# Fetching six tiles of expert outputs and one matrix a stage earlier in a two-layer recurrent and expert kernel

## The chip, the cores and the metric

The kernel runs on one core of one Trainium2 chip. The metric is the device time of one execution in microseconds (us). Engines are named as in the profile: PE (TensorE), PEld (its weight loads), DVE (VectorE), ACT (ScalarE), POOL (GpSimd), SP (SyncE, here a queue for DMAs). Engines tell each other of finished work by semaphores: an instruction or a DMA adds to one, and a queue waits until it has reached a number.

## The reference

Input x has 8 sequences of 512 tokens with 128 features. There are two layers of the form x = x + s * silu(f), both branches from the normalized x.

```python
xn = _layernorm(x)
s = _L0_attn_ref(xn, ...)      # Mamba block: scan, projection, RMS norm, MLP with GELU, RMS norm
g = _silu(_L0_ffn_ref(xn, ...))  # 24 experts, top 2, two expert layers, then layer_norm(out + xn)
x = x + s * g
xn = _layernorm(x)
s = _L1_attn_ref(xn, ...)      # causal attention, 8 heads
g = _silu(_L1_ffn_ref(xn, ...))  # 128 experts, top 2
x = x + s * g
```

The parts at hand are, in layer 0, the end of the Mamba block and the combination of the second expert layer's outputs:

```python
return jnp.einsum('bld,ed->ble', y, out_proj_w)      # end of _mamba
Z_mam = _rmsnorm(y + Z, norm1_w)
h = jax.nn.gelu(jnp.einsum('bld,fd->blf', Z_mam, mlp_w1) + mlp_b1, approximate=False)
return _rmsnorm(jnp.einsum('blf,df->bld', h, mlp_w2) + mlp_b2 + Z_mam, norm1_w)
...
return jnp.einsum('sec,ecf->sf', combine, h)         # end of moe_apply: two rows of two experts per token
...
return layer_norm(out + x, ln_out_w, ln_out_b)
```

## The kernel before

Tokens lie in NT = 32 tiles of P = 128; a batch b (one sequence) has TB = 4 tiles. The program is a row of stages (blocks). In a block each engine has a queue of its own, written as a generator; a block ends when all its engines are through, and only then does the next begin. `side_by_side(main, beside)` weaves two generators on one queue: at each `yield` of the main one it runs the second to its next `yield`, and what is left of the second comes at the end. So the number of `yield`s sets the order of instructions on a queue.

The stages that matter here:

- The scan stage (`scan_stage` with `Moe0Experts` beside it, about 100 to 842 us). DVE scans; PE, ACT, POOL and SP also run both expert layers. SP's queue ends with the stores of expert outputs to `y2_dram` (L1177) and a wait for them (L1180). POOL's queue ends with the gathers of the second layer's inputs (L1222).
- The output stage (`mamba_output_stage` with `Moe0Output` beside it, 842.6 to 1014.6 us). SP loads nine weights (L1512), the normalized rows `xn` in eight parts (L1515) and x (L1516). First phase, b = 0 to 7: PE projects batch b into the one bank `p_o` (L723), DVE adds the rows (L826), which frees the bank, ACT takes squares and roots, DVE scales batch b-1 (L811, L813). After each b DVE combines one pair of tiles: weighted sum of the two gathered rows and the bias product (L1612, L1615), plus `xn`, statistics (L1619 to L1626). PE makes the bias product of four tiles (L1560) after every second projection. Second phase, b = 0 to 7: turn, MLP with GELU, second product, again with one pair of tiles beside each. The end: DVE scales the four quarters of `s_rows` (L811, L813), computes the scale of the second half of the expert branch (`scales(1)`, L1603, L1604), ACT centres it (L1575) and takes SiLU (L1594), DVE weighs (L1639, L1641) and makes the products with s and x (L1648, L1649).
- POOL gathers in that stage, two indirect DMAs for each tile (L1527), into a ring of four tiles `yk`; tile t waits until tile t-4 is combined. PE, ACT and DVE wait for all weights before anything else, POOL before its second tile pair.
- The attention stage (`attention_stage` with `Moe1` beside it, 1057 to 1624 us). 64 heads, two steps each. Beside them run the 128 experts of layer 1; POOL then gathers their outputs (L2220, ring of eight tiles), DVE combines pairs at the steps that begin with `COMBINE_STEP`, ACT takes SiLU at `SILU_STEP`, and from `FINAL_STEP` on DVE makes the final products.

The memory of the rows (`state`) is shared: words 0 to 10752 are the experts' arena during the scan stage, and words 8192 to 12288 are `s_rows`, written in the second phase.

## Time and profile before

| | us |
|---|---|
| median of 3 runs (1626.17 to 1627.29) | 1626.33 |
| the profiled execution: its own time | 1628.29 |
| its span | 1626.5 |
| PE busy | 1348.3 (83%) |
| DVE busy | 1243.7 (76%) |
| ACT busy | 851.8 (52%) |
| POOL busy | 644.9 (40%) |

The span runs from the first instruction to the last. A profile is one execution, and its own time is some microseconds off the median. Busy shares are means over all stages. In a timeline a bracket gives the idle time of the engine before the instruction and what ended it; "issue" is nothing that the profile shows, "remote" an unknown releaser. Ends of matmuls are modelled. PEclk 1.00 is TensorE's granted clock of 2.4 GHz, 0.50 is 1.2 GHz.

### The profile page before, as it was taken

The page shows a single profiled execution, that of the slowest core. Times are in us where ns is not written, and L with a number is a line of the kernel's source. Part 1 is how long each engine was busy: PE and PEld are TensorE (multiplying, and loading weights), DVE is VectorE, ACT ScalarE, POOL GpSimd, SP SyncE. Part 2 cuts the span into 40 slices and gives each one's busy share as a digit, 9 for nine tenths or more (in the row PEclk, how much of TensorE's full clock was granted, in tenths as well). Part 3 has the DMA queues.
Part 4 walks back from the last instruction along what each step waited for, and adds up shares of the span by engine and source line. Part 5 has one row for each costly group of instructions (what it writes and reads, how often), then busy time and mean ns, then how long its engine had stood idle before and what let it go on. Part 6 is the DMA issues. An engine that isn't in the chain of part 4 may idle for free. (4 is left out here: it accounts for less than half of the span.)

```text
span 1626.5 us, 21868 instructions
## 1 busy us (share of the span) xinstructions
PE 1348.3 (83%) x7560; PEld 918.1 (56%) x7560; DVE 1243.7 (76%) x2259; ACT 851.8 (52%) x2096; POOL 644.9 (40%) x592
## 2 busy tenths in 40 slices
PE   7968787879878569898955791589999999798998
PEld 5524444434434348787845561556677677565676
DVE  6669999988898999999956447558887555466667
ACT  5366565656968736565512464743553444333353
POOL 0035655226988664546315440049300221355000
PEclk9978999979898679999977896899999999899999
DMA  6013544443444124545423010300010322112001
GB/s 207 0 30 108 140 137 128 131 135 105 130 129 125 58 80 133 143 126 142 115 77 113 26 27 0 107 1 1 1 53 7 85 82 82 33 36 38 6 14 39
DMA packets 75891, 127.31 MB, mean 78 GB/s; under 512 B 11758, under 2 KB 38606, under 8 KB 75174
## 3 DMA queue, kind: packets, MB, share of 16 engines
q1 hardware_dynamic: 56326, 75.04, 15.3%
q0 software_dynamic: 19456, 50.88, 11.8%
q8 instruction: 61, 1.00, 0.2%
q14 instruction: 48, 0.39, 0.1%
HBM read 85.51 MB, written 40.37 MB: 77 GB/s over the span
## 5 line engine op out<-in xcount | busy, mean ns | idle before, releaser
L643 DVE TENSOR_TENSOR_SCAN sc_st<-sc_dA,sc_st 128x1024 f32<-128x1024 f32 x128 | 293.1, 2330 | 0.0
L2042 DVE COPY at_pT<-at_p_t 128x512 f32<-128x512 f32 (+1 forms) x192 | 109.5, 599 | 147.9 <-PE at_p_t L1935 126.8
L1993 ACT ACTIVATE at_pr<-at_p_s,at_nmx 128x512 f32<-128x512 f32 (+3 forms) x256 | 131.4, 526 | 145.6 <-DVE at_nmx L2019 142.7
L1191 POOL DMA_INDIRECT g_state<-xn_scratch,moe_tab x96 | 116.4, 1212 | 183.0 <-POOLq L99 102.2
L613 DVE TENSOR_TENSOR sc_st<-sc_u,sc_p_b 128x1024 f32<-128x1024 f32 x128 | 154.8, 1210 | 43.2 <-PE sc_p_b L483 20.2
L422 ACT ACTIVATE sc_dA<-sc_dt,g_state 128x511 f32<-128x511 f32 x256 | 169.1, 710 | 16.2 <-DVE sc_st L643 12.7
L1914 PE MATMUL at_p_s<-att_xaT,at_qT 128*128 128x512 f32 (+3 forms) x512 | 175.1, 464 | 0.0
L1948 PEld LDWEIGHTS at_p_o<-at_V,at_pT 128*128 128x128 f32 x1280 | 152.3, 192 | 31.3 <-issue 30.4
L1222 POOL DMA_INDIRECT g_state<-r_scratch,moe_tab x96 | 119.8, 1248 | 108.2 <-PE e_bank L1321 74.1
L1948 PE MATMUL at_p_o<-at_V,at_pT 128*128 128x128 f32 x1280 | 153.8, 275 | 3.1 <-DVE g_state L2032 3.1
L621 DVE TENSOR_TENSOR sc_st<-sc_st,sc_p_c 128x1024 f32<-128x1024 f32 x128 | 155.0, 1211 | 0.0
L513 PEld LDWEIGHTS sc_p_y<-g_ident,sc_st 128*128 128x128 f32 x1024 | 133.9, 154 | 32.6 <-issue 22.1
L513 PE MATMUL sc_p_y<-g_ident,sc_st 128*128 128x128 f32 x1024 | 148.8, 294 | 3.3 <-DVE sc_st L621 3.3
L2019 DVE TENSOR_REDUCE at_nmx<-at_p_s 128x1 f32<-128x512 f32 (+3 forms) x256 | 109.5, 481 | 38.2 <-PE at_p_s L1917 28.1
L483 PE MATMUL sc_p_b<-sc_bc,mamba_sel 96*128 96x512 bf16 x128 | 55.7, 435 | 94.1 <-DVE sc_st L613 86.8
L1201 POOL DMA_INDIRECT g_state<-y_scratch,moe_back x64 | 87.3, 1364 | 84.0 <-DMA y_scratch<-g_state 51.6
L1935 PE MATMUL at_p_t<-g_ident,at_pr 128*128 128x128 f32 x640 | 94.2, 279 | 25.4 <-ACT at_pr L1993 13.1
L1935 PEld LDWEIGHTS at_p_t<-g_ident,at_pr 128*128 128x128 f32 x640 | 75.2, 143 | 65.5 <-DVE at_pT L2042 29.5
L1273 PE MATMUL e_bank<-g_state 128*96 128x512 f32 x192 | 101.6, 631 | 8.0 <-ACT g_state L1335 6.1
L1308 PE MATMUL e_bank<-g_state 128*96 128x128 f32 x768 | 102.2, 277 | 4.4 <-ACT g_state L1442 4.0
L2210 POOL DMA_INDIRECT f_xg<-xn_scratch,l_tab x32 | 30.3, 946 | 184.6 <-DVE l_tab L2418 92.3
L1914 PEld LDWEIGHTS at_p_s<-att_xaT,at_qT 128*128 128x128 f32 x512 | 79.1, 193 | 42.3 <-issue 40.4
(299 smaller groups left out, 2697.6 us busy)
## 6 DMA issues: line engine op xcount, KB each, us to landing
y_scratch<-g_state SPq DMA_DIRECT2D x24, 768.0 KB
g_state<-W SPq DMA_DIRECT2D x48, 256.0 KB
r_scratch<-g_state SPq DMA_DIRECT2D x16, 512.0 KB, 2.6
y_scratch<-g_state SPq DMA_DIRECT2D x24, 192.0 KB
xn_scratch<-g_state SPq DMA_DIRECT2D x16, 256.0 KB, 4.5
g_state<-x SPq DMA_DIRECT2D x4, 512.0 KB, 6.8
g_state<-xn_scratch SPq DMA_DIRECT2D x8, 256.0 KB, 4.6
g_state<-x SPq DMA_DIRECT2D x1, 2048.0 KB, 12.8
```

What stands on the lines that cost most here:

```text
L422: ins = nc.scalar.activation(dA[:, m % 4, j, 1:L], dt[:, b % 2, h, 1:L], ACT.Exp, scale=negA[:, h, 2 * q + j:2 * q + j + 1])
L513: ins = nc.tensor.matmul(p_y[:, t, h * P:(h + 1) * P], st[:, (2 * i + h) % RS, j, t * P:(t + 1) * P], w["ident"], is_transpose=True, start ...
L613: nc.vector.tensor_tensor(st[:, m % RS:m % RS + 2, j, :], u[:, b % 2, :, :], p_b[:, :].unsqueeze(1).broadcast_to([P, HALF, L]), ALU.mult). ...
L621: nc.vector.tensor_tensor(st[:, m % RS, :, :], st[:, m % RS, :, :], p_c[:, :, :], ALU.mult).then_inc(hc_ready, 1)
L643: nc.vector.tensor_tensor_scan(st[:, m % RS, :, :].rearrange("p a b -> p (a b)"), dA[:, m % 4, :, :].rearrange("p a b -> p (a b)"), st[:, ...
L1191: nc.gpsimd.indirect_dma_start(out=self.xg[:, e % 4, h, :], out_offset=None, in_=self.xn_rows, in_offset=bass.IndirectOffsetOnAxis(ap=r.ta ...
L1222: nc.gpsimd.indirect_dma_start(out=self.rg[:, e % 3, h, :], out_offset=None, in_=self.r_rows, in_offset=bass.IndirectOffsetOnAxis(ap=r.tab ...
L1914: nc.tensor.matmul(p_s[:, bank, c:c + K], qT[:, n % 3, i * P:(i + 1) * P], xaT[:, b, 0:K], start=True, stop=False)
L1935: ins = nc.tensor.transpose(p_t[:, bank, c + (i - j) * P:c + (i - j + 1) * P], pr[:, n % 2, sbank, sc + j * P:sc + (j + 1) * P], w["ident"])
L1948: ins = nc.tensor.matmul(p_o[:, i, :], pT[:, n % 2, bank, c + (i - j) * P:c + (i - j + 1) * P], V[:, b % 2, j, h * D:(h + 1) * D], start=( ...
L1993: ins = nc.scalar.activation(pr[:, n % 2, bank, c:c + K], p_s[:, bank, c:c + K], ACT.Exp, bias=nmx[:, n % 2, i:i + 1], accum_out=sums[:, n ...
L2019: ins = v.tensor_reduce(nmx[:, n % 2, i:i + 1], p_s[:, bank, c:c + (i + 1) * P], AX_X, ALU.max, negate=True)
```

## The change

- The memory: a new class `Ahead` takes words 8192 to 10752 of `state`, in which the experts' arena is free once the last outputs are stored: the projection's matrix `out_T` (two tiles) and six tiles of pairs of expert output rows.
- The scan stage: behind the wait for the last stores SP loads `out_T`, and POOL, behind the same waits, issues 12 gathers (tiles 0 to 5).
- The output stage: PE's first wait is for `out_T` alone. The wait for the other eight weights stands before PE's first bias product, before ACT's first GELU work, and on DVE behind the first L826. SP loads two parts of `xn` first, then the weights, then the other six parts. POOL gathers tiles 6 to 27 into a ring of eight without a wait for weights, weighs its first quarter, gathers tiles 28 to 31, and weighs the other three. DVE yields once behind the first quarter of `s_rows`, so that `scales(1)` comes there and no longer behind all four.
- The attention stage: combination begins at step 84, not 80; SiLU at 110, not 108.

```diff
@@ -714,7 +714,7 @@
         block = ctx.enter_context(nc.Block())
 
         def tensor_steps(pe):
-            pe.wait_ge(beside.weights_in, 16 * len(beside.weights))
+            pe.wait_ge(beside.ahead.out_in, 16)
             for b in range(B):
                 if b:
                     pe.wait_ge(o_used, b)
@@ -756,7 +756,6 @@
                 yield
...
         def scalar_steps(act):
-            act.wait_ge(beside.weights_in, 16 * len(beside.weights))
             link = Chain(act, a_chain)
...
@@ -776,6 +775,7 @@
                 roots(slice(b * TB, (b + 1) * TB))
                 yield
             yield
+            act.wait_ge(beside.weights_in, 16 * len(beside.weights))
             for b in range(B):
                 act.wait_ge(z_turned, b + 1)
...
@@ -800,8 +800,6 @@
         def vector_steps(dve):
             link = Chain(dve, chain)
             nc.vector.memset(eps[:, :], 1e-6).then_inc(eps_set, 1)
-            dve.wait_ge(beside.weights_in, 16 * len(beside.weights))
-
...
@@ -824,6 +822,8 @@
                     dve.wait_ge(beside.xn_in[b], 16)
                     dve.wait_ge(projected, b + 1)
                     nc.vector.tensor_tensor(z[:, t, :], rows(p_o), xn_rows[:, t, :], ALU.add).then_inc(o_used, 1)
+                if b == 0:
+                    dve.wait_ge(beside.weights_in, 16 * len(beside.weights))
                 if b:
                     dve.wait_ge(root_ready, b)
...
@@ -841,6 +841,8 @@
             for c in range(4):
                 t = slice(c * 8, (c + 1) * 8)
                 scale(s_rows[:, t, :], t, s_ready)
+                if c == 0:
+                    yield
...
@@ -856,7 +858,7 @@
 
         @block.gpsimd
         def _(pool):
-            side_by_side((None for _ in range(2 * B + 1)), beside.pool(pool))
+            beside.pool(pool)
...
 
+class Ahead:
+
+
+    TILES = 6
+
+    def __init__(self, scope, w, rows, out_T):
+        out_rows = rows[:, 0:HALF * D].rearrange("p (a b) -> p a b", b=D)
+        w["out_T"], self.out_T = out_rows, (out_rows, out_T)
+        self.yk = rows[:, 8 * D:(8 + 2 * self.TILES) * D].rearrange("p (t k d) -> p t k d", k=2, d=D)
+        self.gathered, self.out_in = scope.sem("ahead"), scope.sem("out_in")
+
+
...
     def sync(self, sp):
@@ -1178,6 +1193,7 @@
                          self.out2[:, e % 2, :, :]).then_inc(self.stored2[e % 2], 16)
         for i in range(2):
             sp.wait_ge(self.stored2[i], 16 * (E0 // 2))
+        sp.dma_start(*self.ahead.out_T).then_inc(self.ahead.out_in, 16)
 
     def pool(self, pool):
         nc, r = self.nc, self.r
@@ -1246,6 +1262,14 @@
         for e in range(E0):
             gather_r(e + self.AHEAD)
             yield
+        for i in range(2):
+            pool.wait_ge(self.stored2[i], 16 * (E0 // 2))
+        for t in range(self.ahead.TILES):
+            for k in range(2):
+                nc.gpsimd.indirect_dma_start(
+                    out=self.ahead.yk[:, t, k, :], out_offset=None, in_=self.y2_rows,
+                    in_offset=bass.IndirectOffsetOnAxis(ap=r.back[:, k, t:t + 1], axis=0),
+                ).then_inc(self.ahead.gathered, 16)
...
     HALF_TILES = NT // 2
-
...
     def sync(self, sp):
+        def load_xn(b):
+            t = slice(b * TB, (b + 1) * TB)
+            sp.dma_start(self.xn_rows[:, t, :], self.xn_dram[:, t, :]).then_inc(self.xn_in[b], 16)
+
+        for b in range(2):
+            load_xn(b)
         for dst, src in self.weights:
             sp.dma_start(dst, src).then_inc(self.weights_in, 16)
-        for b in range(B):
-            t = slice(b * TB, (b + 1) * TB)
-            sp.dma_start(self.xn_rows[:, t, :], self.xn_dram[:, t, :]).then_inc(self.xn_in[b], 16)
+        for b in range(2, B):
+            load_xn(b)
         sp.dma_start(self.x_rows[:, :, :], self.x_dram).then_inc(self.x_in, 16)
         sp.wait_ge(self.x_in, 16)
 
     def pool(self, pool):
         nc, r, w = self.nc, self.r, self.w
 
-        def gather(u):
-            for t in range(2 * u, min(2 * u + 2, NT)):
-                if t >= 4:
-                    pool.wait_ge(self.combined, t - 3)
-                for k in range(2):
-                    nc.gpsimd.indirect_dma_start(
-                        out=self.yk[:, t % 4, k, :], out_offset=None, in_=self.y2_rows,
-                        in_offset=bass.IndirectOffsetOnAxis(ap=r.back[:, k, t:t + 1], axis=0),
-                    ).then_inc(self.gathered[t % 4], 16)
-
-        gather(0)
+        def gather(t):
+            n = t - self.ahead.TILES
+            if n >= self.YK:
+                pool.wait_ge(self.combined, t - self.YK + 1)
+            for k in range(2):
+                nc.gpsimd.indirect_dma_start(
+                    out=self.yk[:, n % self.YK, k, :], out_offset=None, in_=self.y2_rows,
+                    in_offset=bass.IndirectOffsetOnAxis(ap=r.back[:, k, t:t + 1], axis=0),
+                ).then_inc(self.gathered[n % self.YK], 16)
+
+        for t in range(self.ahead.TILES, NT - 4):
+            gather(t)
         pool.wait_ge(self.weights_in, 16 * len(self.weights))
-        for u in range(2 * B + 1):
-            gather(u + 1)
-            if u >= B + 2:
-                n = u - B - 2
-                if n % 2 == 0 and n // 2 < 3:
-                    self.weigh_on_pool(pool, n // 2)
-            yield
-        self.weigh_on_pool(pool, 3)
+        self.weigh_on_pool(pool, 0)
+        for t in range(NT - 4, NT):
+            gather(t)
+        for q in range(1, 4):
+            self.weigh_on_pool(pool, q)
...
@@ -1555,6 +1583,8 @@
         for b in range(B):
             if b:
                 pe.wait_ge(self.combined, TB * b)
+            else:
+                pe.wait_ge(self.weights_in, 16 * len(self.weights))
             for j in range(TB):
                 t = b * TB + j
                 ins = self.nc.tensor.matmul(self.bank[:, j * D:(j + 1) * D], gate_rows(self.r.GT, t),
...
@@ -1607,12 +1637,18 @@
         for u in range(2 * B):
             for t in range(2 * u, 2 * u + 2):
                 b, j = divmod(t, TB)
-                dve.wait_ge(self.gathered[t % 4], 32 * (t // 4 + 1))
+                n = t - self.ahead.TILES
+                if n < 0:
+                    y = self.ahead.yk[:, t, :, :]
+                    dve.wait_ge(self.ahead.gathered, 32 * self.ahead.TILES)
+                else:
+                    y = self.yk[:, n % self.YK, :, :]
+                    dve.wait_ge(self.gathered[n % self.YK], 32 * (n // self.YK + 1))
                 dve.wait_ge(self.biased, b + 1)
-                link(v.scalar_tensor_tensor(out=self.o[:, t, :], in0=self.yk[:, t % 4, 0, :],
+                link(v.scalar_tensor_tensor(out=self.o[:, t, :], in0=y[:, 0, :],
                                             scalar=r.wk[:, 0, t:t + 1], in1=self.bank[:, j * D:(j + 1) * D],
                                             op0=ALU.mult, op1=ALU.add))
-                v.scalar_tensor_tensor(out=self.o[:, t, :], in0=self.yk[:, t % 4, 1, :], scalar=r.wk[:, 1, t:t + 1],
+                v.scalar_tensor_tensor(out=self.o[:, t, :], in0=y[:, 1, :], scalar=r.wk[:, 1, t:t + 1],
                                        in1=self.o[:, t, :], op0=ALU.mult, op1=ALU.add).then_inc(self.combined, 1)
             pair = slice(2 * u, 2 * u + 2)
...
@@ -1633,6 +1669,7 @@
             yield
         yield
         scales(1)
+        yield
         for c in (2, 3):
...
@@ -2085,9 +2122,9 @@
     CU = NT // 2
     YK = 8
     COUNT_SLOT, TABLE_SLOT, EXPERT_SLOT = 14, 32, 44
-    EXP_STEP, SILU_STEP = 18, 108
+    EXP_STEP, SILU_STEP = 18, 110
     COUNT_STEP, PICK_STEP, HIGH_STEP, GATE_STEP = 15, 32, 17, 40
-    TABLE_STEP, COMBINE_STEP, FINAL_STEP = 41, 80, 114
+    TABLE_STEP, COMBINE_STEP, FINAL_STEP = 41, 84, 114
...
+        ahead = Ahead(G, w, state[:, 2 * NT * D:Moe0Experts.WORDS], a["out_T"])
...
                 scan_stage(nc, w, xT, z, Arena(state[:, Moe0Experts.WORDS:]), experts)
-            ow = resident(F, ["out_T", "w1_T", "b1", "w2_T", "b2", "norm1", "b2_experts", "ln_out_w", "ln_out_b"])
-            ending = Moe0Output(nc, moe, w, r, y2_dram, xn_dram, xn_rows, s_rows, a["x"], rows, ow)
+            ow = resident(F, ["w1_T", "b1", "w2_T", "b2", "norm1", "b2_experts", "ln_out_w", "ln_out_b"])
```

## Rows read from the trace of the kernel before

**Rows 1.** Part 4 of the page, the chain that ended last, shares of the span by engine.

```profile
PE 23%; DVE 6%; ACT 2%; another core or an unknown queue 2%; issue 1%; ACTq 0%; DVEq 0%
```

**Rows 2.** Windows: stretch, us, busy PE PEld DVE ACT POOL, PEclk, DMA share, GB/s.

```profile
842.60:849.60 7.00, 0.01 (x1) 0.01 (x1) 0.06 (x1) 0.00 (x0) 3.80 (x4) 0.50 0.67 186
849.60:903.00 53.40, 32.94 (x169) 30.64 (x170) 35.28 (x127) 14.10 (x74) 32.09 (x34) 0.72 0.35 118
903.00:984.00 81.00, 70.55 (x376) 49.35 (x376) 33.12 (x101) 43.98 (x120) 35.11 (x34) 0.93 0.09 23
```

**Rows 3.** Waits of DVE, 849 to 903 us: total us, times, longest.

```profile
DVE mo_z L826 <- remote: 12.1, 4, 5.3
```

**Rows 4.** Timeline, 842 to 865 us: start, us, engine, line, operation, [idle before <- releaser].

```profile
842.63 0.36 SPq L1512 DMA_DIRECT2D moe_out_T<-out_T  x1
...
846.21 0.43 SPq L1512 DMA_DIRECT2D moe_ln_out_b<-ln_out_b  x1
...
849.59 3.49 PE L723 MATMUL mo_p_o<-moe_out_T,mamba_xT 128*128 128x128 f32 x16 [7.87 <-DMA moe_ln_out_b<-ln_out_b]
...
856.96 0.17 DVE L1626 TENSOR_SCALAR e_nm<-e_mv 128x2 f32<-128x2 f32 x1
...
859.89 0.69 DVE L826 TENSOR_TENSOR mo_z<-mo_p_o,g_state 128x512 f32<-128x512 f32 x1 [2.76 <-remote]
...
864.34 2.07 PE L1560 MATMUL e_bank<-moe_b_experts,moe_GT 24*128 24x128 f32 x8
...
864.63 0.69 DVE L826 TENSOR_TENSOR mo_z<-mo_p_o,g_state 128x512 f32<-128x512 f32 x1
```

**Rows 5.** Timeline, 866 to 898 us.

```profile
866.35 3.64 PE L723 MATMUL mo_p_o<-moe_out_T,mamba_xT 128*128 128x128 f32 x16
...
869.20 0.17 DVE L1626 TENSOR_SCALAR e_nm<-e_mv 128x2 f32<-128x2 f32 x1
...
872.79 0.69 DVE L826 TENSOR_TENSOR mo_z<-mo_p_o,g_state 128x512 f32<-128x512 f32 x1 [3.42 <-remote]
...
897.59 0.69 DVE L826 TENSOR_TENSOR mo_z<-mo_p_o,g_state 128x512 f32<-128x512 f32 x1
```

**Rows 6.** Timeline, 1396 to 1425 us; the last row is cut by the window.

```profile
1396.10 2.39 PE L1948 MATMUL at_p_o<-at_V,at_pT 128*128 128x128 f32 x20
...
1396.90 0.94 POOL L2220 DMA_INDIRECT f_m<-y_scratch,l_back  x1 [0.31 <-issue]
...
1403.75 2.39 PE L1948 MATMUL at_p_o<-at_V,at_pT 128*128 128x128 f32 x20
...
1418.39 1.29 DVE L2042 COPY at_pT<-at_p_t 128x512 f32<-128x512 f32 x2 [10.27 <-remote]
...
1424.59 0.61 PE L1948 MATMUL at_p_o<-at_V,at_pT 128*128 128x128 f32 x4
```

**Rows 7.** Timeline, 985 to 1014 us.

```profile
985.95 0.20 DVE L811 RECIPROCAL mo_root<-mo_root 128x8 f32<-128x8 f32 x1 [3.04 <-ACT mo_root L770]
...
995.30 0.25 DVE L1603 RECIPROCAL e_rstd<-e_rstd 128x16 f32<-128x16 f32 x1
...
995.79 6.26 ACT L1575 ACTIVATE e_o<-e_o,e_nm,e_rstd 128x128 f32<-128x128 f32 x16 [9.77 <-DVE e_nm L1604]
...
1013.33 1.23 DVE L1649 TENSOR_TENSOR g_state<-g_state,e_o 128x1024 f32<-128x1024 f32 x1
```

**Rows 8.** Waits of all engines, 984 to 1016 us.

```profile
DVE e_o L1639 <- ACT e_o L1575: 3.9, 2, 3.3
```

**Rows 9.** Timeline of POOL, SP and ACT in the scan stage.

```profile
351.49 2.54 POOL L1201 DMA_INDIRECT g_state<-y_scratch,moe_back  x1 [51.63 <-DMA y_scratch<-g_state]
...
822.96 0.30 SPq L1177 DMA_DIRECT2D y_scratch<-g_state  x1
...
841.76 0.60 ACT L402 ACTIVATE mamba_xT<-sc_p_x 128x512 f32<-128x512 f32 x1 [0.81 <-PE sc_p_x L528]
```

**Rows 10.** Waits of SP, 800 to 1062 us.

```profile
SPq L1180 <- DMA y_scratch<-g_state: 2.1, 1, 2.1
```

17 lines of the change are left out of this document (10 added, 7 removed).

## Prediction

> **What bounds the kernel now.** I read the chain that ended last first, then a table of stretches, then the waits of one stretch, then its timeline. By the chain most of the end is made by TensorE in the last stage [rows 1]. A stage starts only when every engine has left the stage before it. So what the change does in the stage that ends the first layer (842.6 to 1014.6) counts in full if it moves that stage's last instruction, and not at all otherwise.
>
> In that stage no engine is full [rows 2]: in the projection phase (849.6 to 903) PE is busy for 32.9 us of 53.4, DVE for 35.3, POOL for 32.1 with 34 gathers. The phase is a ring: PE projects a batch, DVE adds the rows (L826) and frees the bank, PE projects the next. The reader should look for the gathers, because the change is about them: DVE never waits at L1612, the first instruction that reads a gathered tile. All that it waits for inside the phase is L826, four times, 12.1 us, put down to nothing that the profile knows [rows 3]. The timeline says more [rows 4, 5]. The load of the weights is waited for by PE until 849.59. The second L826 starts at 859.89 although DVE was free at 857.13 and its rows had long been asked for. The fourth starts at 872.79, DVE free at 869.37, while the projection that it needs ended at 869.99 by the profile's model of matmuls. The common part is a PE result whose signal is late. It happens while POOL issues gathers one after the other, a gather being 0.94 us and 0.30 us between two. The same is seen in the last stage: behind a burst of gathers one head of attention takes 20.8 us (1403.75 to 1424.59) where the head before it took 7.65, with DVE idle for 10.27 us at once [rows 6]. I call this the lateness. I do not know its mechanism; I take its price from these rows.
>
> After the last square root (985.95) DVE bounds the stage: four quarters of s_rows, the scale, then it waits 3.9 us for ScalarE's centring, which could not start before 995.79, because DVE made the scale last [rows 7, 8].
>
> **The change part by part.**
>
> *Start of the stage.* PE no longer waits for the weights at its first projection, and it can start at about 842.7 in place of 849.59. But it then meets the wait for the weights before the first bias product, which stands ahead of the second projection in its queue, and DVE meets it after the first L826, ahead of the first pair. So the wait is not removed but set one instruction further. Nine DMAs stood from 842.63 to 846.21, so 0.45 us each; the last one landed 3.4 us behind its issue [rows 4]. Now two loads of rows come first and one weight less: the last issue is 0.45 us later, and the landing near 850.1. The loads ahead of it bring 512 KB and take away 128: at the 186 GB/s of this stretch [rows 2] the 384 KB more are 2.1 us if nothing overlaps. I take 0.4, so 850.5 (range 850.1 to 852.2). Then the bias product at the lower clock level (1.2 GHz, the granted clock being 0.50 while PE waited), 2.07 us [rows 4], to 852.6, and the second projection at that level, 3.64 [rows 5], to 856.2. DVE's pair starts at 852.6 and is a part of its step of 4.74 us (859.89 to 864.63, [rows 4]), so it is done by then. The second L826 thus comes at 856.3 against 857.1 without lateness: gain 0.8 us (855.9 to 858.0 by the landing's range: from 1.2 gained to 0.9 lost). Of PE's seven microseconds little is left.
>
> *Gathers and ring.* Since DVE waited for no gather, neither the six tiles fetched ahead nor the ring of eight removes a wait by itself. What they change is POOL's pattern. A ring of four tiles stopped POOL again and again (34 gathers at one in 1.25 us are 42 us, in 53.4). Now the stage begins with 16 in a row (tiles 6 to 13, 843.3 to 863), then it waits until eight tiles are combined. Lateness per gather in the phase before is 12.1/34 = 0.36 us [rows 2, 3]. By 850.5 about 6 of the new ones are out; up to the eighth L826 fourteen tiles are combined, so tiles up to 21 are asked for: 32 gathers, 26 of them beside PE's work, 9.3 us at that rate. The first burst is longer, so I take 10.0: gain 2.1 us. Bounds: no lateness, gain 12.1; and the first burst at the price of the burst in rows 6, 20.84 - 7.65 = 13.2 us in place of the 2.76 of the second L826, so loss 10.4. PE's tail of the phase and the phase behind it (903 to 984), whose PE is busy for 70.6 of 81.0 us [rows 2], move with the eighth L826 (897.59, [rows 5]) and keep their length; POOL's first weighing now stands behind tile 27 and before 28, and its inputs are ready far earlier. The late sign of a projection has no place in the Trainium skill: its page "TensorE: Matmul & The Clock Gate", section "The cost: per-tile semaphore tail", gives under 0.1 us for the signal behind one group of matmuls. By that rule none of the stalls would be PE's, and the rival in which lateness goes would be the forecast; the trace disagrees, with 2.8 us between the projection's end at 869.99 and DVE's start at 872.79 [rows 5].
>
> *Scan's end.* POOL and SP now wait for the last store of expert outputs, issued at 822.96 and landed by about 825.4 (0.30 and the 2.1 of SP's wait, [rows 9, 10]); nothing is queued behind either wait in that stage but the new DMAs themselves. SP's one load costs nothing. POOL's twelve gathers take 12 x 1.25 = 15 us, to 840.2; the stage ends at 842.36 with ScalarE's last copy [rows 9], so they fit with 2 us. That cover can go: a gather beside DVE's scan instructions took 2.54 us in place of 0.94 [rows 9], and two such instructions lie here; two stretches of 1.6 make 843.3, 0.9 too late. A late signal on the serial way from DVE's last sums over PE's two turns to ScalarE would add 2.76. I take 0.8 (0 to 3.7). The Trainium skill's page "SBUF — State Buffer", section "Who interferes with whom", has the pair of ports that GpSimd and VectorE share locked for a whole instruction. The stretched gather fits that; if every gather waited out a scan in this way, POOL would set this stage's end, which by the rows is the 0.9.
>
> *End of the stage.* A quarter of s_rows takes (995.30 - 985.95)/4 = 2.34 us, the scale 0.49 [rows 7]. With the scale behind the first quarter ScalarE starts at 988.8 and its 6.26 us are over at 995.1; DVE is busy with the other three quarters to 995.8 and finds both halves ready. Its 3.9 us of waiting [rows 8] are gone, less 0.1: gain 3.8 us (3.0 to 3.9). SiLU needs ScalarE from 995.1, earlier than before, and the last product follows as DVE runs; DVE is the cover and is full until the end.
>
> *Second combination.* Four steps later are two heads. The burst of 16 gathers hangs on the stores of expert outputs, not on the step, and stays; the other 48 gathers move from some heads to others of the same kind, and the last combination still comes four steps before SiLU and eight before the final products. Nothing is removed: 0. Since lateness falls where it falls, I allow a third of the 13.2, 4 us, to both sides.
>
> **Sum.** -0.8 - 2.1 + 0.8 - 3.8 + 0 = -5.9 us. The profiled execution's own time is 1628.29 us, with 1.8 us around its span of 1626.5, and lies 2.0 above the median of 1626.33. So 1622.4 for a profiled execution, 1620.4 for the median.
>
> **The rivals.**
> - *Lateness as before, chance 0.50:* the forecast, 1616 to 1624.5.
> - *Lateness goes, 0.17.* If it hangs on the short ring (POOL restarting when DVE frees a tile), the ring of eight takes it away: -0.8 - 12.1 + 0.8 - 3.8 = -15.9, 1610.4. For it: all four stalls lie in a phase with a short ring. Against it: the burst of attention [rows 6] had a ring of eight and was the worst.
> - *The gain in front is taken back, 0.20.* Each longer run of gathers holds PE's signals a little more (lateness 14 to 18 in place of 10), which eats the 3.8 of the stage's end: 1624.5 to 1629.
> - *Slower, 0.13.* The first 16 gathers cost what the burst of attention cost. The place is the second and third L826, near 856 to 866; the price 13.2 against 2.76. Then lateness is 9.3 + 13.2 = 22.5, and the time -5.9 + 12.5, 1632.9. It decides from a lateness of 10 + 5.9 + 3.3 = 19 us on. For it: equal number, equal spacing of gathers. Against it: PE works less densely here (32.9 of 53.4 us), and it waits for weights during the first 7 us.
> - *The change does nothing in front.* That is part of the forecast, in which the front is worth only 0.8 us.
>
> **How the numbers follow.** A measurement of this kernel tells 0.2%, 3.3 us: faster is below 1623.1, slower above 1629.6. The forecast's case lies below 1623.1 with 0.42 of its 0.50, the second wholly; of the third most is same, of the last most slower. Faster 0.60, same 0.25, slower 0.15. Eight times in ten: 1610 to 1630.
>
> **What the profile would show.** Right: the first L826 near 846 and the second near 856; DVE idle between for the weights; twelve gathers between 825 and 842 and the next stage's start within 1 us of 842.6; L1603 some 2.4 us behind the first L811 of the end; no wait at L1639; L1612 without waits as before. Wrong: L826 waits that sum to under 5 or over 16 us; a scan stage that ends after 844; heads of attention between 40 and 54 that are longer in sum than before by more than 4 us.

## The result, and the profile after

Slower by 0.9%: 1640.03 us, the median of 4 runs (1637.91 to 1641.92), against 1626.25, the median of 4 (1614.16 to 1627.29); ratio 1.0093, 95% interval 1.0058 to 1.0128. The forecast was 1620.4, its range ended at 1630. The profiled execution after took 1640.71 us (span 1638.9), before 1628.29 (span 1626.5): 12.4 us to account for.

Five landmarks, in us, read from the rows below and from [rows 4, 5, 7]:

| stretch | before | after | difference | forecast |
|---|---|---|---|---|
| up to SP's first load of the output stage | 842.63 | 852.80 | +10.2 | +0.8 |
| from there to the eighth sum of rows (L826, now L824) | 54.96 | 57.54 | +2.6 | -2.9 |
| to the first reciprocal of the end | 88.36 | 87.95 | -0.4 | 0 |
| to the last sum into `x_rows` (L1649, now L1686) | 27.38 | 23.33 | -4.05 | -3.8 |
| to the end of the span | 613.17 | 617.28 | +4.1 | 0 (4 to both sides) |

The first line is most of it. Timeline of the changed kernel around the scan's end, some rows of all engines (start, us, engine, line, operation; in brackets the idle time before and what ended it):

```profile
825.85 0.96 POOL L1269 DMA_INDIRECT g_state<-y_scratch,moe_back  x1 [24.79 <-DMA y_scratch<-g_state]
...
829.62 2.64 POOL L1269 DMA_INDIRECT g_state<-y_scratch,moe_back  x1 [0.30 <-issue]
...
832.57 1.87 POOL L1269 DMA_INDIRECT g_state<-y_scratch,moe_back  x1 [0.30 <-issue]
...
840.90 0.63 PE L528 MATMUL sc_p_x<-g_ident,scan_z 128*128 128x128 f32 x4 [0.78 <-issue]
...
842.24 0.94 POOL L1269 DMA_INDIRECT g_state<-y_scratch,moe_back  x1 [0.30 <-issue]
...
852.80 0.82 SPq L1538 DMA_DIRECT2D g_state<-xn_scratch  x2
...
852.88 0.06 DVE L802 MEMSET mo_eps<- 128x1 f32 x1 [13.47 <-PEq L317]
...
853.44 0.94 POOL L1557 DMA_INDIRECT e_yk<-y_scratch,moe_back  x1 [10.26 <-POOLq L317]
```

The twelve gathers do what the forecast said, two of them stretched beside DVE's scans, and the last is over at 843.18. PE is through at 841.5. Nothing computes after 843.2, yet the next stage starts at 852.8. What runs in the gap is an instruction of POOL's sequencer, which the timeline leaves out and the view of one source line shows. Line 317 closes the stage (duration min/median/max in ns, then first and last start in us), changed kernel:

```profile
L317 POOLq EVENT_SEMAPHORE  x2: 17/17/17, 852.6 to 852.7; - x2
...
L317 POOLq DRAIN  x1: 21968/21968/21968, 830.6 to 830.6; - x1
L317 DVEq DRAIN  x1: 1256/1256/1256, 838.2 to 838.2; - x1
L317 PEldq DRAIN  x1: 658/658/658, 840.9 to 840.9; - x1
L317 ACTq DRAIN  x1: 627/627/627, 841.6 to 841.6; - x1
```

POOL's DRAIN, with which it leaves the stage, lasts from 830.6 to 852.6 and ends 9.4 us behind its last gather. ScalarE, PE and DVE leave by 842.2. The kernel before has the same row:

```profile
L317 POOLq DRAIN  x1: 14057/14057/14057, 795.6 to 795.6; - x1
```

There it ended at 809.7, 8.4 us behind the last gather (800.38 and 0.92) and 33 us before anybody waited for it. So the price stood in the trace of before, and the forecast read the gathers beside it and not this row.

The projection phase of the changed kernel, DVE's sums and PE:

```profile
856.39 0.69 DVE L824 TENSOR_TENSOR mo_z<-mo_p_o,g_state 128x512 f32<-128x512 f32 x1 [3.45 <-PE mo_p_o L723]
...
876.08 0.69 DVE L824 TENSOR_TENSOR mo_z<-mo_p_o,g_state 128x512 f32<-128x512 f32 x1 [9.57 <-remote]
...
880.82 0.69 DVE L824 TENSOR_TENSOR mo_z<-mo_p_o,g_state 128x512 f32<-128x512 f32 x1
...
895.61 0.69 DVE L824 TENSOR_TENSOR mo_z<-mo_p_o,g_state 128x512 f32<-128x512 f32 x1 [0.60 <-remote]
...
905.60 0.69 DVE L824 TENSOR_TENSOR mo_z<-mo_p_o,g_state 128x512 f32<-128x512 f32 x1 [5.28 <-remote]
...
910.34 0.69 DVE L824 TENSOR_TENSOR mo_z<-mo_p_o,g_state 128x512 f32<-128x512 f32 x1
```
```profile
852.85 3.43 PE L723 MATMUL mo_p_o<-g_state,mamba_xT 128*128 128x128 f32 x16 [11.32 <-PEq L317]
861.45 2.07 PE L1590 MATMUL e_bank<-moe_b_experts,moe_GT 24*128 24x128 f32 x8 [5.17 <-DMA moe_ln_out_b<-ln_out_b]
863.45 3.78 PE L723 MATMUL mo_p_o<-g_state,mamba_xT 128*128 128x128 f32 x16
```

The first sum comes 3.6 us behind the stage's start in place of 10.6, and PE then waits 5.17 us for the last weight, as forecast. That weight is in 8.65 us behind the stage's start (forecast 7.9), and the second projection is over at 867.2 by its model, 14.4 us behind the start (forecast 13.7). But DVE goes on only at 876.08. POOL's rows:

```profile
872.18 0.94 POOL L1557 DMA_INDIRECT e_yk<-y_scratch,moe_back  x1 [0.30 <-issue]
888.43 0.94 POOL L1557 DMA_INDIRECT e_yk<-y_scratch,moe_back  x1 [15.31 <-DVE e_o L1651]
```

The run of 16 gathers without a pause (853.44 to 873.12) ends 3 us before DVE goes on. The timeline calls what ended DVE's wait "remote", that is, unknown. But the trace also holds the updates of the semaphores: the one by which PE tells of the second projection stands at 875.95, the last one recorded of the rows' landing at 856.38, and the last of the sixteen matmuls started at 866.81. So it was PE's sign that came late, not the rows. Since ends of matmuls are modelled, a late sign can't be told from a last matmul that ended late; "late sign" stands for both here. In all the lateness is 15.4 us in 3 waits, against 12.1 in 4 [rows 3] and the 10.0 of the forecast.

The end of the stage, changed kernel (L809 is L811 of before, L1633 is L1603):

```profile
998.29 0.20 DVE L809 RECIPROCAL mo_root<-mo_root 128x8 f32<-128x8 f32 x1 [3.04 <-ACT mo_root L769]
...
1000.63 0.25 DVE L1633 RECIPROCAL e_rstd<-e_rstd 128x16 f32<-128x16 f32 x1
...
1001.12 6.26 ACT L1605 ACTIVATE e_o<-e_o,e_nm,e_rstd 128x128 f32<-128x128 f32 x16 [2.76 <-DVE e_nm L1634]
...
1021.62 1.23 DVE L1686 TENSOR_TENSOR g_state<-g_state,e_o 128x1024 f32<-128x1024 f32 x1
```

The scale starts 2.34 us behind the first reciprocal (in [rows 7] 9.35), and the stage's end is 4.05 us nearer.

### The profile page after: what moved, and what is told of

The parts are those of the page before. It is cut to its first block and busy times, and to the rows that moved or that the text cites. A ratio compares the mean times of both kernels' runs of the same rounds, so it can differ in the third digit from the quotient of the medians.

```text
span 1638.9 us, 21870 instructions
## 1 busy us (share of the span) xinstructions
PE 1345.9 (82%) x7560; PEld 916.5 (56%) x7560; DVE 1244.8 (76%) x2259; ACT 851.9 (52%) x2096; POOL 642.1 (39%) x592
## 5 line engine op out<-in xcount | busy, mean ns | idle before, releaser
L1238 POOL DMA_INDIRECT g_state<-r_scratch,moe_tab x96 | 114.2, 1189 | 113.9 <-PE e_bank L1345 79.7
```

## The experiments

Eighteen kernels ran in six sets (the expectations say "call"); the kernels of a set ran on one chip, beside the same runs of the kernel before. The sets fell into two groups. In two (e9 and e10; e17 and e18) the kernel before took 1629 to 1630 us, near the 1626 of the comparison above. In the other four (e1 to e4, e5 to e8, e11 and e12, e13 to e16) it took 1588 to 1591, and no profile of those shows a late sign of PE in the output stage or in attention. The first group ran on chips 5 and 15, the second on chips 14, 13, 14 and 11, so the chip may be the difference; no run shows it.

One thing more is needed to read them: most kernels, the one before too, take some 10 to 17 us less in some of their executions. In the profiles this is made in the scan stage (e12's output stage starts at 827.3, e15's at 842.3, and from there to the end they take 732.8 and 732.6 us). So times of stages are given from the stage's own start, and a median of few runs can lie between the two kinds. The ratios are those on record, which are not quotients of the medians.

| run | kernel | us | before in its set | ratio (95%) |
|---|---|---|---|---|
| e1 | no tile ahead | 1581.15 | 1588.33 | 0.9961 (0.9931 to 0.9992) |
| e2 | four tiles ahead | 1586.87 | 1588.33 | 0.998 (0.995 to 1.0011) |
| e3 | changed, with marks | 1592.07 (one run) | 1588.33 | |
| e4 | before, with the scale early | 1583.03 | 1588.33 | 0.9972 (0.9938 to 1.0007) |
| e5, e13 | changed kernel | 1592.26, 1592.1 | 1589.0, 1588.02 | 1.0032 (0.9994 to 1.007), 1.0028 (0.999 to 1.0066) |
| e6 | two tiles ahead | 1581.89 | 1589.0 | 0.9972 (0.994 to 1.0004) |
| e7 | none ahead, ring of four | 1582.34 | 1589.0 | 0.9964 (0.9932 to 0.9996) |
| e8 | before, second combination later | 1588.03 | 1589.0 | 1.0012 (0.998 to 1.0044) |
| e9 | none ahead, one late write of POOL | 1642.84 | 1629.46 | 1.0105 (1.003 to 1.0181) |
| e10 | two ahead, biases first | 1629.27 | 1629.46 | 1.0023 (0.999 to 1.0057) |
| e14 | the same | 1577.86 | 1588.02 | 0.9941 (0.9905 to 0.9977) |
| e12, e15 | the same, ring of four | 1571.25, 1576.74 | 1590.66, 1588.02 | 0.9897 (0.9855 to 0.9939), 0.995 (0.9911 to 0.9988) |
| e17 | the same, ring of four | 1622.63 | 1629.74 | 0.9958 (0.9927 to 0.999) |
| e11, e16 | e10 with four gathers in the stage | 1577.09, 1576.05 | 1590.66, 1588.02 | 0.9928 (0.9903 to 0.9954), 0.9942 (0.9902 to 0.9982) |
| e18 | the same | 1607.07 | 1629.74 | 0.9891 (0.9842 to 0.994) |

### What holds the end of the scan stage

**e1, no tile ahead.**

```diff
-    TILES = 6
+    TILES = 0
```

> The changed kernel with no tile fetched ahead: POOL's first 16 gathers of the output stage are tiles 0 to 7, and no gather stands in the last 17 us of the scan. Theory A (POOL's burst of gathers just before a stage's end holds back the end, by POOL or by another engine's signal): the output stage starts at 842.5 in place of 852.8, and the time is 10 us below the changed kernel's 1640.0, so 1630. Rival B (the hole from 843 to 852.8 was an accident of the one profiled run): the time stays within 3 us of the changed kernel's, 1637 to 1643, whatever the profile shows. Rival C (the lateness of the following stage depends on how many gathers remain for it): 12 gathers more beside PE's projections give back 12 x 0.36 = 4.3 us, so 1634.

The output stage started at 843.0, 0.3 us behind ScalarE's last copy, and the time was 11 us below the changed kernel's 1592.2 of the same group (a comparison between sets; e6 repeats it within one). Theory A, not B. C's price, 4.3 us, is too small, and no sign was late here for it to work on.

**e2, four tiles** (`TILES = 4`).

> The changed kernel with four tiles fetched ahead in place of six: 8 gathers at the scan's end, the last one at about 837 to 838.5, PE's last transposes at 841.5 and ScalarE's last copy at 842.2 as before. A1 (POOL can leave a stage only a fixed time, 9.4 us, after its last gather): the next stage starts at 847 to 848. A2 (POOL works off a backlog that grows with the number of gathers, 9.4 us for 12): 6.3 us behind the last one, at 844 to 845. A3 (what is late is the sign of PE or another engine, held only while gathers are being issued): none is issued in the last 3 us, so 842.5.

The last gather was over at 839.38, ScalarE's last copy at 843.3, and the stage started at 848.67. A3 is out, since no gather had been issued for 9 us, and so is A2, which has 844 to 845. POOL's DRAIN:

```profile
L317 POOLq DRAIN  x1: 18433/18433/18433, 830.0 to 830.0; - x1
```

It ended at 848.4, 9.05 us behind the last gather. That is nearest to A1, if 0.7 us later than it has it, but the time isn't quite fixed: 9.05 with eight gathers, 9.38 with twelve. More on this below.

**e3, marks.**

```diff
+        pool.wait_ge(self.ahead.gathered, 32 * self.ahead.TILES)
+        nc.gpsimd.memset(self.ahead.mark[:, 0:1], 0.0)
...
+            dve.wait_ge(y_turned, 2 * B)
+            nc.vector.memset(beside.ahead.mark[:, 1:2], 0.0)
+            dve.wait_ge(yT_ready, 2 * B)
+            nc.vector.memset(beside.ahead.mark[:, 2:3], 0.0)
```

> The changed kernel, and three tiny writes that leave marks in the trace at the scan's end: POOL writes one column after it has waited for its twelve gathers to land (about 844.7), DVE one behind PE's last transposes (about 841.6) and one behind ScalarE's last copy (about 842.2). A1 or A2 (POOL itself is held, by a fixed time or a backlog): POOL's mark stands at 852 or so, or it stands at 844.8 and the stage then ends right behind it, because the wait has taken the place of the held end. A3 (another engine's sign is held): POOL's mark at 844.8, and the stage still ends near 852.8; if DVE's marks are at 841.6 and 842.3 too, the sign held is that of leaving the stage and no matmul's.

```profile
839.60 0.06 DVE L661 MEMSET g_mark<- 128x1 f32 x1 [2.19 <-PE sc_p_x L528]
...
840.23 0.06 DVE L663 MEMSET g_mark<- 128x1 f32 x1 [0.57 <-ACT mamba_xT L402]
...
840.23 0.94 POOL L1274 DMA_INDIRECT g_state<-y_scratch,moe_back  x1 [0.30 <-issue]
...
842.84 0.10 POOL L1279 MEMSET g_mark<- 128x1 f32 x1 [1.67 <-DMA g_state<-y_scratch,moe_back]
...
852.56 0.82 SPq L1545 DMA_DIRECT2D g_state<-xn_scratch  x2
```
```profile
L317 POOLq DRAIN  x1: 9495/9495/9495, 842.8 to 842.8; - x1
```

PE's and ScalarE's signs are in time. POOL is free too: it computes at 842.84, as soon as its gathers have landed. Then its DRAIN takes 9.5 us. The times are those that A3 expected, but its reading falls: the engine held is POOL, not in its work, as A1 and A2 had it, but in leaving, and not for the gathers' landing. The Trainium skill's page "PSUM — Partial Sum Buffer", section "Engine vs sequencer instructions", has it that a drain waits for the engine to go fully idle; that names the instruction, and no 9 us for an engine that was ready for other work.

**e6, two tiles** (`TILES = 2`).

> The changed kernel with two tiles fetched ahead in place of six: four gathers, the last one over at 831 to 833. Theory A1 (the DRAIN with which POOL leaves a stage ends 8.4 to 9.4 us behind its last gather): it ends at 840 to 842, PE and ScalarE are the last to leave as in the kernel before, the output stage starts at 842.5 to 843 and the time is 9 to 10 us below the changed kernel's of this call. A2 (a share per gather) would give the same here, but not the 848.7 seen with eight gathers. Rival: any gather at the scan's end costs the stage 5 us or more; then it starts at 848 or later.

```profile
L317 POOLq DRAIN  x1: 14017/14017/14017, 826.2 to 826.2; - x1
```

It ended at 840.2, before ScalarE's copy (841.4), and the stage started at 841.7, so in time. The kernel took 10.4 us less than e5 in the same set. A1, and the size of the term: all of it goes with the place of POOL's last gather.

**e9, one write of POOL at the end and no gather there.**

```diff
+            pool.wait_ge(y_turned, 2 * B - 1)
+            nc.gpsimd.memset(beside.ahead.mark[:, 0:1], 0.0)
```

> The changed kernel with no gather at the scan's end (no tile ahead), and one tiny write of POOL behind PE's first turn of the last batch, at about 841. In four profiles of kernels with gathers at that place POOL's DRAIN ended 8.7 to 9.4 us behind its last instruction, a gather or (9.38) the mark's write behind the gathers' landing. Theory A4 (whatever POOL does last in a stage, its DRAIN then takes 8 to 9.4 us): the output stage starts at 849.5 to 850.5 in place of 843.0, and the time is 6 to 8 us above that of the kernel with no tile ahead. Rival A5 (only the gathers make the DRAIN long, and these ended 40 us earlier): the stage starts at 843 and the time is that of the kernel with no tile ahead.

```profile
L317 POOLq DRAIN  x1: 8508/8508/8508, 839.6 to 839.6; - x1
```

A write of 0.10 us at 839.57, 39 us behind POOL's last gather, and the stage starts at 848.4 in place of some 841.8 (ScalarE's last copy being over at 841.5). So A4, not A5, though 1.1 us earlier than A4's range: the last instruction of any kind sets where the DRAIN begins to count. In e1, where POOL came to its DRAIN at 826.0 after 24 us without work, it lasted 8.4 us all the same. The time can't be set against e1's, which ran in the other group. In the kernel before the DRAIN of the stage behind the output stage, in which POOL does nothing, took 0.04 us:

```profile
L1664 POOLq DRAIN  x1: 40/40/40, 1016.1 to 1016.1; - x1
```

**What sets its length** can be read from all 20 profiles together: the number of gathers that POOL issued in the stage, early or late.

| stage | profiles | gathers of POOL in the stage | DRAIN's end behind POOL's last instruction, us |
|---|---|---|---|
| output | e11, e16, e18 | 4 | 0.41 |
| output | changed, e3, e5, e13 | 52 | 4.33 |
| output | e2 | 56 | 4.65 |
| output | two tiles ahead and all gathers | 60 | 4.98 |
| output | before, e1, e4, e7, e8, e9 | 64 | 5.31 |
| attention | all | 96 | 7.90 |
| scan | before, e4, e8, e9 (e1, e7: from its start) | 256 | 8.40 |
| scan | two tiles ahead | 260 | 8.73 |
| scan | e2 | 264 | 9.05 |
| scan | changed, e3, e5, e13 | 268 | 9.38 |

In the output stage POOL's last instruction is the same `tensor_tensor` of 1.27 us, and its DRAIN starts with it; the kernel before and e18:

```profile
L686 POOLq DRAIN  x1: 6612/6612/6612, 978.0 to 978.0; - x1
```
```profile
L686 POOLq DRAIN  x1: 1712/1712/1712, 954.9 to 954.9; - x1
```

In the output stage and in the scan stage a gather more makes the tail 0.08 us longer. In the output stage that is all of it, and its line, carried on to 96 gathers, gives the 7.90 of attention (an estimate from these rows). In the scan stage it isn't: by that line 256 gathers would make 21 us, where 8.40 were measured, and no run shows why. What the last instruction is makes no difference (9.38 behind e3's write, 9.38 behind e5's gather). So A2 was right in kind and wrong in what it counted: the twelve gathers brought 1.0 us of the tail, and 8.4 had stood there before.

### The parts alone

**e4, the scale early**, added to the kernel before: a `yield` behind the first quarter of the scale of s_rows and one behind `scales(1)`.

> The kernel before with one part of the change: DVE makes the second half's scale behind the first quarter of s_rows in place of behind the fourth. By the forecast's step it is worth 3.8 us (3.0 to 3.9): no wait of 3.9 us for the centring, the output stage's end at 1010.7 in place of 1014.5, and the time 1622.5 against 1626.3. Rival: ScalarE's earlier start moves nothing, because the last combinations wait for something else behind it: time within 1 us of the kernel before.

First reciprocal at 961.92, last sum at 985.24: 23.32 us in place of 27.38 [rows 7]. The median was 5.3 us lower; the interval just includes 1, so it is the stage and not the whole time that shows the gain.

**e8, the second combination four steps later** (`COMBINE_STEP` 84, `SILU_STEP` 110), in the kernel before.

> The kernel before with one part of the change: the second combination four steps later, SiLU two. Forecast's step: nothing is removed, 0, and up to 4 us either way through the lateness of heads of attention. Without lateness: within 1 us of the kernel before. Rival: the later combination runs into the end, and the time is 2 us or more above.

The median was 1.0 us lower, the ratio 1.0012 (0.998 to 1.0044): nothing to be seen where no sign is late.

**e5 and e7.** e5 is the changed kernel; e7 has no tile ahead and `YK = 4`.

> The changed kernel itself, once more, beside the others of this call. In the runs so far the kernel before took 1588 us in place of 1626 and the profiles of its variants showed no late sign of PE at all. By theory A (POOL's leaving, a DRAIN of 9.4 us behind its last gather, costs 10.2 us at the scan's end, the rest of the change gains): where the lateness is absent, the start of the output stage gains 4 us and its end 4, so the ratio to the kernel before is (10.2 - 8)/1588 above 1, 1.001 to 1.002, and where it is present, 1.009 as in the first comparison. Rival: the 1.009 has a cause in the last stage, and stays in either case.

> The changed kernel with no tile ahead and with a ring of four tiles again in place of eight. Forecast's step (the ring removes no wait by itself, what it changes is the pattern of POOL's gathers and with it the lateness): without lateness the same time as the kernel with no tile ahead and the ring of eight, within 1 us, seven steps of 4.75 us in the projection phase. Rival (the ring of four holds DVE: DVE waits for gathers once nothing else is late): the phase is 2 to 5 us longer, with waits of DVE at the first combination of a tile.

e5: ratio 1.0032, where 1.001 to 1.002 was expected without lateness and the interval takes in both. The 10 us of the DRAIN are there too, and something more: from the stage's start to the eighth sum it needs 44.7 us, e6 42.4. Table of stretches, e5, then e6, then e13, the same kernel as e5 (after the stretch and its length: busy time of PE, PEld, DVE, ACT and POOL, then the granted clock, DMA share and GB/s):

```profile
851.70:897.00 45.30, 35.45 (x160) 32.72 (x160) 30.90 (x110) 12.31 (x64) 28.51 (x30) 0.59 0.48 154
```
```profile
841.70:885.00 43.30, 28.65 (x160) 26.27 (x160) 31.15 (x111) 12.45 (x65) 32.65 (x34) 0.77 0.51 167
```
```profile
840.60:885.90 45.30, 30.62 (x160) 27.95 (x160) 32.23 (x115) 13.59 (x72) 29.49 (x31) 0.69 0.48 155
```

PE came to e5's phase from 11.3 us of idling and ran more of it at the lower of its two levels (1.2 and 2.4 GHz; a projection takes 3.78 us at the one, 2.05 at the other). It is tempting to say that a DRAIN that keeps PE waiting is paid for again behind it, but the runs don't show that: e13 had the same 11.3 us of idling and needed 43.2 us to the eighth sum, and e7 idled for 0.94 and needed 44.1. What varies is the share of the phase at the lower level, and what sets that is open. e7's 44.1 us against e1's 42.4 lie between the forecast's 1 us and the rival's 2 to 5, with no wait of DVE for a gather. Its sums are later from the second one on (15.6 us behind the start, e1's 13.9): PE waited 6.21 us for the last weight in place of 4.71. e2, with the ring of eight, waited 6.12, so this need not be the ring's doing.

### The late signs

**e10, a version from these runs:** two tiles ahead; and the experts' biases loaded first and waited for alone.

```diff
-    TILES = 6
+    TILES = 2
...
-                pe.wait_ge(self.weights_in, 16 * len(self.weights))
+                pe.wait_ge(self.bias_in, 16)
...
-                if b == 0:
+                if b == 1:
```

(The last line is DVE's wait for the other weights; PE's stands ahead of `hidden(0)`. The lines that put the biases first in SP's queue and give them a semaphore of their own aren't shown.)

> A version of the changed kernel made from what the runs showed: two tiles ahead in place of six, so that POOL's DRAIN ends before PE and ScalarE do; and the experts' biases loaded first of the weights, PE's first bias product waiting for them alone, the others waited for by DVE at its first scale and by PE ahead of the hidden layer. In the profile of the kernel with two tiles ahead PE waits 4.7 us for the last weight (ln_out_b) before the first bias product, with the second sum of rows 10.3 us behind the first. Theory: these 4.7 us are on the path, the second sum comes 6 to 7 us behind the first, and the time is 3.5 to 4.5 us below the kernel with two tiles ahead, 12 below the changed kernel. Rival: the landing of the rows or the scale's wait for its weight takes the place, and less than 1 us is gained.

It fell into the group with late signs and gained nothing over the kernel before. Its profile showed why; rows of DVE, PE and POOL:

```profile
833.90 0.69 DVE L825 TENSOR_TENSOR mo_z<-mo_p_o,g_state 128x512 f32<-128x512 f32 x1 [3.49 <-DMA g_state<-xn_scratch]
...
852.37 0.69 DVE L825 TENSOR_TENSOR mo_z<-mo_p_o,g_state 128x512 f32<-128x512 f32 x1 [13.65 <-remote]
```
```profile
835.68 2.05 PE L723 MATMUL mo_p_o<-g_state,mamba_xT 128*128 128x128 f32 x16
...
853.11 3.79 PE L723 MATMUL mo_p_o<-g_state,mamba_xT 128*128 128x128 f32 x16 [15.38 <-DVE mo_z L825]
```
```profile
849.67 0.95 POOL L1559 DMA_INDIRECT e_yk<-y_scratch,moe_back  x1 [0.30 <-issue]
855.23 0.94 POOL L1559 DMA_INDIRECT e_yk<-y_scratch,moe_back  x1 [4.62 <-DVE e_o L1653]
```

The projection is over at 837.7 and PE, DVE and ScalarE stand still from 839 on, until POOL's run of 16 gathers ends at 850.6; 1.7 us later DVE goes on. e9 says the same: a run of 20 gathers over at 873.7, DVE's second sum at 874.51 after a wait of 13.35. Without late signs the biases are worth it: e14's second sum came 8.3 us behind its start, e6's 13.8, and the eighth 38.6 against 42.4.

**e12 (ring of four), e11 (four gathers).** Both are e10's version with one thing changed. Theory L is that a sign waits for the end of POOL's run.

```diff
-    YK = 8
+    YK = 4
```

> The same version (two tiles ahead, biases first) with a ring of four tiles in place of eight, so that POOL's first run in the output stage is 8 gathers, over about 10 us behind the stage's start, in place of 16, over after 20. Theory L (a sign of PE waits for the end of the run): the second sum comes 10 to 12 us behind the stage's start in place of 22, the eighth at 50 to 54 in place of 58.9, and the time is 5 to 9 us below that of the version with the ring of eight, where signs are late; where none is, the same within 1.5 us. Rival M (lateness has nothing to do with the length of a run): the same time as with the ring of eight in either case.

```diff
-        for t in range(self.ahead.TILES, NT - 4):
+        for t in range(self.ahead.TILES, self.ahead.TILES + 2):
             gather(t)
...
-        for t in range(NT - 4, NT):
-            gather(t)
```

> The version with two tiles ahead and the biases first, but POOL issues only four gathers in the output stage in place of 60: the tiles from the fifth on are combined from the two tiles gathered last, so this part of the computation is left out. Theory L (PE's signs are held while POOL issues gathers back to back; in the profile of that version the second projection ended at 837.7 by its model, the run of 16 gathers at 850.6, and DVE went on at 852.4, 13.7 us idle): with the gathers gone no wait of DVE for a sign of PE is longer than 1 us after the second sum, the second sum comes 6 to 7 us behind the first in place of 18.5, and all eight in 40 us in place of 55.3. Rival M (the signs are late through the loads of rows and weights, or through PE itself): the stage's waits stay, 10 us or more between the first and the second sum beyond the 6. Where no sign is late at all (as in the calls in which the kernel before took 1588), the run tells only that 60 gathers cost nothing there.

(e11 and e18 also take the tiles from the fifth on from the last two gathered; those lines aren't shown. Their result is wrong for that reason, and what follows the output stage works on other values.) No sign was late in this set, nor in the next (e13 to e16, the same kernels together):

> The changed kernel itself, as the base of this call. Where signs are late (kernel before at 1626 to 1629): 1640, the output stage's start near 852.5 and the second sum of rows 20 us or more behind it; where none is late: 1592, ratio 1.003.

> Two tiles ahead, biases first, ring of eight. Where signs are late: 1629 as in its first call, the second sum at the end of POOL's run of 16 gathers, 22 us behind the stage's start. Where none is late, by the theory that the wait for the last weight was on the path: second sum 10 us behind the stage's start and 3.5 us below the kernel with two tiles ahead, so 1578.

> The same with a ring of four: first run of 8 gathers. Theory L (a sign waits for the end of the run): where signs are late, the second sum 10 to 12 us behind the stage's start, 5 to 9 us below the ring of eight of this call. Rival M: the same time as with the ring of eight. Where none is late: within 1.5 us of the ring of eight.

> The same with four gathers in the output stage in place of 60 (the tiles from the fifth on are combined from the last two gathered: left out). Theory L: where signs are late, none longer than 1 us is left in the output stage after the second sum, and the stage's projection phase takes 40 to 42 us. Rival M: the second sum is as late as with the ring of eight, 20 us behind the start.

There the ring makes no difference (1577.86 and 1576.74) and 60 gathers cost next to nothing (1576.05 without 56 of them; the eighth sum 37.0 us behind the start in place of 38.6). e14 met its expectation for the time (1578), and its second sum came 8.3 us behind the start where 10 was expected. e12's median of 1571.25 lies between the two kinds of its six executions, three at 1561 to 1564 and three near 1579, while only one of the eleven of the kernel before was below 1585; so its ratio is too good, and e15's 0.995 is the one to use.

**e17 and e18** fell into the group with late signs.

> Two tiles ahead, biases first, ring of four. If the kernel before takes 1626 to 1629 in this call: by theory L (a sign of PE waits for the end of POOL's run of gathers) the first run is of 8, the second sum comes 10 to 12 us behind the stage's start in place of 22 with a run of 16, and the time is 5 to 9 us below the 1629 of the ring of eight; by rival M (the length of the run has no part in it) the second sum is 18 us or more behind the start and the time 1627 to 1631. If the kernel before takes 1588: 1577, and it tells nothing of this.

> The same with the ring of eight and four gathers in the output stage in place of 60 (the other tiles are combined from the last two gathered: left out). Where signs are late: by theory L no wait for a sign of PE over 1 us in the output stage, its eight sums within 40 to 42 us of its start; by rival M the second sum as late as with 60 gathers, 22 us behind the start. Where none is late: 1576.

Sums of e17, then the end of its first run:

```profile
846.15 0.69 DVE L825 TENSOR_TENSOR mo_z<-mo_p_o,g_state 128x512 f32<-128x512 f32 x1 [3.50 <-DMA g_state<-xn_scratch]
...
854.76 0.69 DVE L825 TENSOR_TENSOR mo_z<-mo_p_o,g_state 128x512 f32<-128x512 f32 x1 [4.16 <-remote]
```
```profile
851.97 0.94 POOL L1559 DMA_INDIRECT e_yk<-y_scratch,moe_back  x1 [0.30 <-issue]
857.63 0.94 POOL L1559 DMA_INDIRECT e_yk<-y_scratch,moe_back  x1 [4.72 <-DVE e_o L1653]
```

And of e18:

```profile
844.95 0.69 DVE L825 TENSOR_TENSOR mo_z<-mo_p_o,g_state 128x512 f32<-128x512 f32 x1 [3.49 <-DMA g_state<-xn_scratch]
...
849.73 0.69 DVE L825 TENSOR_TENSOR mo_z<-mo_p_o,g_state 128x512 f32<-128x512 f32 x1
...
854.47 0.69 DVE L825 TENSOR_TENSOR mo_z<-mo_p_o,g_state 128x512 f32<-128x512 f32 x1
```

Times behind the stage's start are counted from DVE's first instruction in it (L802 or as in the fences):

| group with late signs | first run of gathers | second sum behind the run's end | second sum behind the stage's start | eighth |
|---|---|---|---|---|
| before | broken by a wait for weights | | 17.2 | 54.9 |
| changed | 16 | 3.0 | 23.2 | 57.5 |
| e9 | 20 | 0.9 | 26.1 | 62.7 |
| e10 | 16 | 1.7 | 22.0 | 58.9 |
| e17 | 8 | 1.8 | 12.2 | 53.9 |
| e18 | 4 | no wait | 8.3 | 37.0 |

Rival M falls, and theory L holds for the long waits. (e17's 12.2 us are just past the 10 to 12 expected, e18's 37.0 below the 40 to 42; rival M had 18 or more and 22 for the second sum.) With the gathers gone the phase is as short as in the other group (e16: 37.0). With them it is 17 us longer with the ring of four (e17) and 22 with the ring of eight (e10). In these profiles DVE waited eleven times for over 3 us for a sign of PE, and each of these waits ended 0.3 to 3.0 us behind the end of a run of 8 to 20 gathers. Between the rings lie 6.6 us of time (1629.27 and 1622.63, two sets, with the kernel before at 1629.46 and 1629.74), within the 5 to 9 expected.

Theory L isn't the whole rule, though. By the updates of PE's semaphore the eight signs of each of the 14 profiles without lateness stand 0.01 or 0.02 us behind the modelled end of the projection, also within runs of 52 gathers. In the other group most signs of projections that ended within 3 us of a run's start stand there too, in the midst of the run (changed kernel: 856.29, 889.94, 910.14), and those that ended 4.7 us or more into it are 0.6 to 14.5 us late. Some late ones arrived before the run was over (changed kernel: 895.49, 2.4 us late, the run lasting to 903.2). What decides between them is open.

## Why the prediction was wrong

- **Scan's end: the step that failed.** Twelve gathers take 15 us and "fit with 2 us", so 0.8 us (0 to 3.7); it was 10.2. The gathers themselves went as forecast: the last was over at 843.18, where two stretched ones had given 843.3. What was left out is that POOL must leave the stage as well, and its DRAIN in that stage ends 8.4 to 9.4 us behind its last instruction, or behind its own start where POOL had long been idle (all 20 profiles). The bound of 3.7 came from a stretched gather and a late sign; the nearest row, POOL's DRAIN of 14.06 us in the same stage of before, was not among the rows read. With the forecast's own 843.3 for the last gather and the 8.4 us of that row the stage had ended at 851.7, some 9.2 us late, and the sum had been -5.9 - 0.8 + 9.2 = +2.5; with the measured 10.2 it is +3.5.
- **Gathers and ring: the mechanism stood in the rows, the size was wrong.** Forecast was a lateness of 10.0 us, a gain of 2.1, with a loss of 10.4 as the bound; it measured 15.4, a loss of 3.3. Lateness per gather (0.36 us) was the wrong unit. The long waits last to the end of the run, so what counts is the length of the run that is under way when PE finishes. The first run of 16 was over 20 us behind the stage's start, and the second projection 14.4 behind. That is a wait of 9.6 in place of 2.76. The rival "slower" had this place and this cause, at a price of 13.2; it was given 0.13 and did not know of the DRAIN, without which it had not come about by itself: 2.6 - 0.4 - 4.05 + 4.1 = +2.2 us is no slower than before by the bound of 3.3. "Against it: PE waits for weights during the first 7 us" was true and didn't help, the run being longer than that.
- **Start of the stage: the mechanism was right, the gain about nothing.** It hung on the weights, not on PE's start. The last weight came 8.65 us behind the start in place of 7.9, and the second projection ended at 14.4 us in place of 13.7, where without lateness the kernel before would have had its second sum at 14.5 (857.1); so the 0.8 gained was not there, inside the bounds of 1.2 gained to 0.9 lost. e14 confirms it from the other side, with 5.5 us gained to the second sum when the bias product no longer waits for the last weight.
- **End of the stage: right,** 4.05 us for 3.8 (its range ended at 3.9), and 4.06 alone in e4.
- **Second combination: at the edge of its bound,** +4.1 for 0 with 4 to both sides. The last gathers of the changed kernel end 27 us later (1533.5 in place of 1506.4), with late signs up to 1535. That the 4.1 come from this is not shown: e8 has none of it, but ran where no sign is late.
- **What would have made it wrong** was named rightly: a scan stage ending after 844. L824's waits were 15.4 us, inside the 5 to 16. The other sign, heads of attention longer by more than 4 us, can't be told from the 4.1 above.

Where no sign is late, the smaller parts of the change all but pay for the DRAIN: the same kernel is at 1.003 there, which can't be told from 1. The version that came out of the runs keeps these parts, with two tiles ahead, the biases first and the ring of four: 0.9958 (e17, with late signs), 0.995 and 0.9897 (e15 and e12, without; e12's is too good, as said above). None of the three intervals reaches 1.

## What to carry to other kernels

Work put into an engine's slack at the end of a stage must end earlier than the others' work by what that engine needs to leave: read its DRAIN row, and not only its last instruction, and expect that row to grow with the gathers that the engine issues in the stage. And a long unbroken run of gathers is a cost of its own where signs are late behind it: a deeper ring lengthens the run, so let the ring's depth be no more than the consumer needs. A fetch that nobody waits for gains nothing by coming earlier: with no tile ahead the kernel took 1581.15 us (e1), with two 1581.89 (e6).

## What the runs showed of the hardware

- POOL's DRAIN: 8.4 us in the scan stage even where POOL had been idle for 24 (e1), and an end 8.4 to 9.4 behind its last instruction otherwise; 0.04 us where POOL did nothing (before). Its tail grows by 0.08 us with each gather of the stage: 0.41 us with 4, 4.33 with 52, 5.31 with 64, 7.90 with 96, and 8.40 with 256 to 9.38 with 268.
- Late signs of PE while POOL issues gathers, with waits up to 13.7 us, in all profiles of one group (e18 in attention only) and in none of the other. The Trainium skill's "TensorE: Matmul & The Clock Gate", section "The cost: per-tile semaphore tail", has a formula that gives 0.06 us for one array tile and one increment (an estimate by it), and 126 ns measured for sixteen tiles. The 0.11 us between the modelled end of the changed kernel's first projection and DVE's first sum agrees; the late signs have no place in it. The runs show that the gathers are needed for the lateness in the output stage and that the long waits end with their run. They don't show through what the sign is held, nor what the two groups differ in besides the chips. Of the 38 to 42 us between their times for the same kernel, 9 lie between the output stage's start and the eighth sum (54.9 before, 45.6 in e8, whose front is that of before), and 25 behind the first PE instruction of line 1760 (1021.7 to the end, 604.8 us, and 579.8 in e8), where attention has late signs in the one group and none in the other.
- The scan stage is some 10 to 17 us shorter in some executions of most kernels, in both groups (before, beside e5 to e8: 8 runs at 1573 to 1579 among 27 at 1587 to 1594). The cause is open.
